# A transformer layer with routed experts on one core: two units share one routed part, norms are split between ACT and POOL, products fill a wait of PE

## The chip, the cores and the metric

The kernel runs on one core of a Trainium2 chip. The metric is the device time of one execution, in microseconds (us); lower is better. Three runs of the kernel before took 269.41, 272.25 and 278.97 us, median 272.25 us. The change is judged against that median.

## The reference, cut to what matters

All arithmetic is float32, on x of 4 batches of 1024 tokens of 64 features.

```
q, k, v = x@Wq+bq, x@Wk+bk, x@Wv+bv
y = ((d_gamma * (q @ k.T)) @ v) @ Wo + bo        # per batch, 1024 x 1024, no softmax
h = where(y >= 0, y, a*y)
n = layernorm(h)                                  # state-space block, 128 states
u = (1-A) * (n@Wb+bb) * (n@Wx+bx),  A = exp(-softplus(n@Wd+bd))
s_t = A_t * s_(t-1) + u_t                         # scan over the 1024 tokens
h = h + ((n@Wc+bc) * s) @ Wy + by
n = layernorm(h)                                  # 16 experts, top 2 by a gate
p = softmax(n@gate_w + gate_b);  top 2, renormalised
h = h + sum over the 2 experts of p_e * (silu(n@w1_e) * (n@w2_e)) @ w3_e
```

## The kernel before, in words

The tokens are cut into four **units** of 1024 rows each (two batches by half of the tokens: `UNITS`, `unit_of`). Every unit goes through attention (8 steps; a step is a product `scores`, L699, a multiplication on DVE, `mix`, L1029, and a product `pv`, L713), then through a chain: `center1`, sums of squares and their root, `turn_norm`, four products of the state-space block (`product`, L739), the scans on DVE, `ssm_out` (L768), and then `center2` (L774, with the raw gate logits, L778), the second norm, the choice of two experts, `count` and `place`.

Each engine runs one instruction queue in program order and waits on semaphores. The order is written out by hand: a loop over **beats** (`for m in range(BEATS)`); two beats are one attention step. `BEAT` gives each operation of a unit its beat after the end of the unit's last step (first number; the second one is for the last unit), and `due(name, m)` says for which units it is due. The chain of unit u thus lies among the attention steps of unit u+1.

The first three units are **routed**: `place` and `give_slots` work out for each token and each of its two experts a slot in a buffer in device memory. A part's buffer has 32 blocks of 128 slots: one block that belongs to each of the 16 experts (own blocks) and 16 that are handed out to whichever expert overflows (shared blocks, `SHARED = 2 * UT`). POOL scatters the normed rows into the slots (`scatter`, L490, 16 indirect transfers a unit), SP loads four blocks at a time (`load_slots`, L379), and this **group** of four blocks goes through PE as `turn_slots` (L822), `hidden` (L858) and, three groups later, `result` (L881). ACT does the silu (L587) and moves results out (L593), DVE multiplies (`gated`, L1158), SP stores results (L400), and POOL gathers them back (`gather`, L499, again 16 transfers a unit). Before, each routed unit is a part of its own: `PARTS = 3`, 8 groups a part, `ROUTED = 24` groups. The owners of the shared blocks are worked out in `spread`, `owner_rows` and `owners`; SP loads the weights of shared blocks by these numbers (`load_weights`, L394).

The last unit is **dense**: all 16 experts on all rows, in 32 groups (`hidden_dense`, L904, and `result_dense`, L916), after the routed groups. Its rows are first multiplied with the share that each expert gets (`weigh`, L1170), which SP spreads over the partitions through device memory (`spread_given`, L414, eight transfers of 512 KB).

A group is cut into four **pieces** (`expert_piece`). From beat `FFN_BEAT` on, `FFN_RATES` says how many pieces are run in each beat among the last unit's chain; what is left runs after the beats. SP stores results 7 groups behind the load (`STORE_LAG`), but only 4 behind at the first group of a part in `LATE_PARTS`. POOL's order is three scatters and then three gathers (`POOL_ORDER`). `COMBINE_AFTER` gives the groups behind which DVE adds gathered results (`combine`, L1193 to L1195).

A second norm before: ACT squares 512 columns into `squares` (L531), DVE sums them (`norm_var`, L1039), ACT takes the root (L535), DVE takes the reciprocal and scales the rows into `n2` (`norm_scale`, L1049).

Of the kernel before, what the change touches and what calls it, by code (L numbers as in the profile page):

```python
# [14 lines left out]
P = 128  # L15
# [15 lines left out]
PARTS = UNITS - 1  # L31
OWN, SHARED = NE, 2 * UT
BLOCKS = OWN + SHARED
GB = 4
PAIRS = GB // 2
GROUPS = BLOCKS // GB
OWN_GROUPS = OWN // GB
SHARED_GROUPS = SHARED // GB
ROUTED = PARTS * GROUPS

# [15 lines left out]
    "relu": (0, 0), "sq1": (2, 2), "std1": (2, 3), "tanh_table": (3, 9), "turned": (9, 6), "tanh": (9, 7),  # L56
    "keep": (13, 8), "half": (26, 21), "sqrt_table": (12, 13), "sq2": (17, 14), "std2": (18, 14), "h": (21, 13),
    "center1": (3, 2), "turn": (6, 6), "d": (7, 7), "x": (9, 8), "b": (10, 9), "c": (12, 11), "out": (15, 13),
    "center2": (17, 14), "turn_h": (22, 11), "count": (25, 18), "owner_row": (32, 24), "prelu": (2, 1),
    "var1": (4, 3), "scale1": (5, 3), "xs": (9, 8), "bx": (11, 9), "scan0": (13, 9), "scan1": (13, 11),  # L60
    "read": (13, 11), "residual": (15, 11), "var2": (18, 13), "scale2": (19, 14), "logits": (20, 14),
    "mark0": (21, 15), "one0": (22, 15), "mark1": (23, 15), "one1": (23, 17), "place": (25, 18), "slots": (27, 18),
    "spread": (31, 19), "owners": (33, 26), "weights": (33, 20), "x_turn": (1, 20), "dispatch": (0, 22),
    "given_turn": (1, 23),
# [3 lines left out]
PV_LAG = 3  # L68
# [23 lines left out]
COMBINE_AFTER = (29, 31, 40, 47, 49, 53)  # L92
# [32 lines left out]

def out_order():
    order = []
    routed = [("routed", r, m) for r in range(PARTS) for m in range(COMBINES)]
# [10 lines left out]
def build_layer(nc, xT, dgT, wqk, vecs, wssm, wgate, rows, wvo, wy, w12, w3, out):  # L139
    with ExitStack() as ctx:  # L140
# [6 lines left out]
        slots_dram = [nc.dram_tensor(f"slots{r}", [BLOCKS * P, D], F32).ap() for r in range(PARTS)]  # L147
        given_dram = nc.dram_tensor("given", [BH, NE, CW], F32).ap()
        results_dram = [nc.dram_tensor(f"results{r}", [BLOCKS * P, D], F32).ap() for r in range(PARTS)]
# [6 lines left out]
        mixed = sb("mixed", [P, 2, BH, CW])  # L156
# [40 lines left out]
        block_at = sb("block_at", [SHARED, NE])  # L197
        iota_i = sb("iota_i", [P, NE], I32)
# [12 lines left out]
        first_slot = sb("first_slot", [P, NE])  # L211
        slot_f = sb("slot_f", [P, 2, UT])
        slot_i = sb("slot_i", [P, PARTS, 2, UT], I32)
        is_past = sb("is_past", [SHARED, NE])
        owner_col = sb("owner_col", [SHARED, 1])
        owner_i = sb("owner_i", [1, PARTS * SHARED], I32)
# [10 lines left out]
        back_v = sb("back_v", [P, PARTS, UT, 2, D])  # L227
# [46 lines left out]
        diff_done, half_done = sem("diff_done"), sem("half_done")  # L274

        scattered = [sem(f"scattered{i}") for i in range(PARTS)]
# [5 lines left out]
        gathered = [sem(f"gathered{i}") for i in range(PARTS * COMBINES)]  # L282
# [53 lines left out]
        def _(sp):  # L336
# [46 lines left out]
            def load_weights(r, i):  # L383

                if i == 0:
                    sp.wait_ge(owner_done, r + 1)
                k = r * SHARED_GROUPS + i
# [3 lines left out]
                if r >= 1:  # L391
                    sp.wait_ge(hid_done, (r - 1) * GROUPS + OWN_GROUPS + i + 1)
# [4 lines left out]
            def store_results(n):  # L397
                r, g = divmod(n, GROUPS)
# [20 lines left out]
            for n in range(ROUTED):  # L419
                r, g = divmod(n, GROUPS)  # L420
# [5 lines left out]
                if 1 <= g <= SHARED_GROUPS:  # L426
                    load_weights(r, g - 1)
# [26 lines left out]
        def _(pool):  # L454
# [22 lines left out]
            link(pool.memset(first_slot[:, 0:1], 0.0))  # L477
            link(pool.memset(chosen[:, UT, :], 0.0))
            link(pool.iota(iota_i[:, 0:NE], [[-1, NE]], NE, 0))
            link(pool.tensor_copy(rank_of[:, :], iota_i[:, 0:NE]))  # L480
            link(pool.iota(iota_i[:, 0:NE], [[P, NE]], 0, P))
            pool.tensor_copy(block_at[:, :], iota_i[0:SHARED, 0:NE]).then_inc(consts, 1)

            def scatter(r):
                pool.wait_ge(zeroed, 16 * PARTS)
                pool.wait_ge(norm_done[1], r + 1)
                pool.wait_ge(slot_done, r + 1)
                for i in range(UT):
                    for k in range(2):
                        pool.indirect_dma_start(  # L490
                            out=slots_dram[r], out_offset=bass.IndirectOffsetOnAxis(ap=slot_i[:, r, k, i:i + 1], axis=0),
                            in_=n2[:, r % 2, i, :], in_offset=None).then_inc(scattered[r], 16)

            def gather(r):
                for i in range(RES_BUFS):
                    pool.wait_ge(stored[i], 16 * ((r + 1) * GROUPS // RES_BUFS))
# [810 lines left out]
```

## Time and profile before

| | |
|---|---|
| median of three runs | 272.25 us (269.41 to 278.97) |
| the profiled execution, its own time | 265.82 us |
| its span, first to last instruction | 264.1 us |
| PE busy | 242.3 us (92%) |
| DVE busy | 164.2 us (62%) |
| ACT busy | 104.4 us (40%) |
| POOL busy | 98.7 us (37%) |
| mean granted clock of PE | 0.947 |

The page shows busy shares over the whole span. PE is busy nearly throughout, but busy is not full speed: the row PEclk, over 40 slices of 6.6 us, shows 5 in four slices from 185 us on in tenths of full speed. The queries by stretch and by time, of which rows stand below, say where that begins and what PE did before it.

### The profile page before, as it was taken

How to read it: one execution, taken by the hardware profiler on the slowest of the kernel's cores; microseconds unless marked ns; L12 is line 12 of the kernel's file. 1: busy time of each engine (PE TensorE's matmuls, PEld its weight loads, DVE VectorE, ACT ScalarE, POOL GpSimd, SP SyncE). 2: the span in 40 equal slices, each digit the busy share in tenths (PEclk: the TensorE clock that was granted, in tenths of full speed). 3: DMA queues.
4: the chain of work that ended last, by engine and by line, in shares of the span. 5: the costliest groups of instructions: out<-in, count | busy, mean ns of one | idle time of the engine just before them, and what ended most of it. 6: DMA issues, size and time to landing. Idle time of an engine off the chain costs nothing.

```text
span 264.1 us, 4634 instructions
## 1 busy us (share of the span) xinstructions
PE 242.3 (92%) x1641; PEld 143.3 (54%) x1641; DVE 164.2 (62%) x289; ACT 104.4 (40%) x186; POOL 98.7 (37%) x119
## 2 busy tenths in 40 slices
PE   8999999999999999966999899599999978999994
PEld 7642224224422442235768688488888644565661
DVE  1354366598999998978695854111214479765773
ACT  2212234603570347037838846323234233334341
POOL 5000000000006774477407777772377517770000
PEclk9999999999999999999999999955559999999999
DMA  5999990000000001434135466554799952112001
GB/s 162 354 381 386 249 206 14 0 0 1 2 0 10 25 27 39 117 100 123 35 84 128 135 158 145 124 135 118 156 242 236 240 125 54 38 25 45 22 21 40
DMA packets 46373, 29.73 MB, mean 113 GB/s; under 512 B 33072, under 2 KB 41456, under 8 KB 45840
## 3 DMA queue, kind: packets, MB, share of 16 engines
q1 hardware_dynamic: 43280, 26.30, 38.5%
q0 software_dynamic: 3072, 3.15, 4.9%
q8 instruction: 13, 0.21, 0.3%
q14 instruction: 8, 0.07, 0.1%
HBM read 20.46 MB, written 8.98 MB: 111 GB/s over the span
## 4 chain that ended last, share of the span: by engine, by line
PE 64%; DVE 16%; issue 8%; DMA 5%; ACT 5%; DVEq 0%; SPq 0%; POOL 0%; ACTq 0%; POOLq 0%
PE ring L858 10%; PE ring L699 9%; PE acc L713 9%; PE turn L881 9%; PE ring L904 7%; DMA results<-res 4%; PE side L739 3%; PE turn L916 3%; DVE state L1070 3%; DVE mixed L1029 2%; DVE dg L1170 2%; PE side L672 2%; PE ring L656 2%; PE acc L822 2%; DVE act L1158 2%
## 5 line engine op out<-in xcount | busy, mean ns | idle before, releaser
L490 POOL DMA_INDIRECT slots<-n,slot_i x48 | 48.1, 1003 | 105.4 <-DVE slot_i L1134 91.7
L1158 DVE TENSOR_TENSOR act<-ring,silu 128x512 f32<-128x512 f32 x56 | 38.5, 688 | 52.0 <-ACT silu L587 51.2
L499 POOL DMA_INDIRECT back_v<-results,slot_i x48 | 46.6, 972 | 31.2 <-DMA results<-res 17.5
L587 ACT ACTIVATE silu<-ring 128x512 f32<-128x512 f32 x56 | 33.3, 597 | 48.9 <-PE ring L904 28.9
L1029 DVE TENSOR_TENSOR mixed<-ring,dg 128x1024 f32<-128x1024 f32 x32 | 39.0, 1218 | 11.8 <-PE ring L699 11.6
L699 PE MATMUL ring<-kq 64*128 64x512 f32 x128 | 35.5, 631 | 0.0
L713 PE MATMUL acc<-mixed,v 128*64 128x512 f32 x128 | 34.5, 617 | 0.6 <-ACT nT L522 0.4
L881 PE MATMUL turn<-w_sb,act 128*128 128x64 f32 (+1 forms) x192 | 31.7, 317 | 1.2 <-ACT res L593 0.9
L881 PEld LDWEIGHTS turn<-w_sb,act 128*128 128x128 f32 x192 | 28.1, 225 | 7.2 <-issue 5.8
L904 PE MATMUL ring<-nT,w_sb 64*128 64x256 f32 x128 | 21.7, 415 | 3.5 <-DVE dg L1170 2.7
L699 PEld LDWEIGHTS ring<-kq 64*128 64x128 f32 x128 | 10.1, 185 | 19.7 <-issue 14.5
L739 PE MATMUL side<-nT,wssm_sb 64*128 64x512 f32 x64 | 17.5, 625 | 3.4 <-ACT nT L543 1.4
L904 PE MATMUL ring<-dg,w_sb 64*128 64x256 f32 x128 | 19.1, 376 | 0.0
L858 PE MATMUL ring<-slots_t,w_sb 64*128 64x128 f32 x192 | 17.5, 334 | 0.8 <-DVE act L1158 0.8
L713 PEld LDWEIGHTS acc<-mixed,v 128*64 128x64 f32 x128 | 6.4, 134 | 21.2 <-issue 15.6
L521 ACT ACTIVATE hT<-acc,vec 128x512 f32<-128x512 f32 x4 | 2.7, 687 | 37.3 <-PE acc L713 37.3
L858 PEld LDWEIGHTS ring<-slots_t,w_sb 64*128 64x128 f32 x192 | 15.0, 233 | 3.9 <-issue 2.8
L904 PEld LDWEIGHTS ring<-nT,w_sb 64*128 64x128 f32 x128 | 10.3, 185 | 12.4 <-DVE dg L1170 8.1
L593 ACT ACTIVATE res<-turn 128x256 f32<-128x256 f32 x24 | 9.2, 383 | 19.7 <-PE turn L881 16.8
L858 PE MATMUL ring<-slots_t,w_shared 64*128 64x128 f32 x192 | 16.3, 317 | 0.1
L858 PEld LDWEIGHTS ring<-slots_t,w_shared 64*128 64x128 f32 x192 | 13.9, 217 | 2.5 <-issue 2.4
L822 PE MATMUL acc<-ident,slots 128*128 128x128 f32 x48 | 11.0, 315 | 2.8 <-DMA slots<-slots 2.8
(144 smaller groups left out, 290.2 us busy)
## 6 DMA issues: line engine op xcount, KB each, us to landing
dg<-dgT SPq DMA_DIRECT2D x8, 512.0 KB, 7.6
dg<-given SPq DMA_DIRECT2D x8, 512.0 KB, 10.2
slots<-zeros SPq DMA_DIRECT2D x3, 1024.0 KB, 13.4
slots<-slots SPq DMA_DIRECT2D x24, 128.0 KB, 2.8
w_shared<-w SPq DMA_DIRECT2D x48, 64.0 KB, 2.1
results<-res SPq DMA_DIRECT2D x24, 128.0 KB, 2.7
w_sb<-w SPq DMA_DIRECT2D x2, 1024.0 KB, 14.5
xs<-xT SPq DMA_DIRECT2D x4, 256.0 KB, 6.4
```

The lines of the kernel that those rows point to most:

```text
L490: pool.indirect_dma_start(out=slots_dram[r], out_offset=bass.IndirectOffsetOnAxis(ap=slot_i[:, r, k, i:i + 1], axis=0), in_=n2[:, r % 2, i ...
L499: pool.indirect_dma_start(out=back_v[:, r, i, k, :], out_offset=None, in_=results_dram[r], in_offset=bass.IndirectOffsetOnAxis(ap=slot_i[: ...
L587: s.activation(silu[:, n % 2], hidden_banks(n)[:, :, 0:PAIRS * P], ACT.Silu).then_inc(silu_done, 1)
L699: mm = pe.matmul(ring[:, 2 * (step % 2) + b, :], kq[rows_b(b), hh, 0, j * P:(j + 1) * P], kq[rows_b(b), hh, 1, th * CW:(th + 1) * CW], sta ...
L713: mm = pe.matmul(acc[rows_b(b), :], v[:, u // 2, j, b, :], mixed[:, step % 2, b, :], start=j == 0, stop=j == JT - 1)
L739: mm = pe.matmul(side[:, b, :], wssm_sb[rows_b(b), col:col + CH], nT[rows_b(b), :], start=True, stop=True)
L822: mm = pe.transpose(slots_bank[:, q * P:(q + 1) * P], slots[:, n % SLOT_BUFS, 2 * q:2 * q + 2, :].rearrange("p n d -> p (n d)"), ident[:, :])
L858: mm = pe.matmul(hidden_banks(n)[:, b, c:c + P], w[:, part * HID:(part + 1) * HID], slots_t[rows_b(b), n % 2, q, :], start=True, stop=True)
L881: mm = pe.matmul(result_bank(n)[:, k * D:(k + 1) * D], act[:, n % ACT_BUFS, k % 2, k // 2 * P:(k // 2 + 1) * P], w, start=True, stop=True)
L904: mm = pe.matmul(hidden_banks(n)[:, b, part * PAIRS * P:(part + 1) * PAIRS * P], w12_sb[rows_b(b), e, part * HID:(part + 1) * HID], x, sta ...
L1029: dve.tensor_tensor(mixed[:, step % 2], ring[:, r:r + 2, :], dg[:, u % 2, j, :].unsqueeze(1).broadcast_to([P, BH, CW]), ALU.mult).then_inc ...
L1158: dve.tensor_tensor(act[:, n % ACT_BUFS], hidden_banks(n)[:, :, PAIRS * P:2 * PAIRS * P], silu[:, n % 2], ALU.mult).then_inc(act_done, 1)
```

## The change

Units 0 and 1 become one routed part. Its buffer keeps 16 own blocks and has 32 shared ones, 12 groups; unit 2 is the second part with 8 groups. `ROUTED` falls from 24 to 20, `ALL_GROUPS` from 56 to 52. Unit 1's tokens go on filling the blocks that unit 0 began (`room`, `past_own`, `moved`, `is_behind`). `load_slots` of the first part waits for the scatters of both units. In detail:

- For units 0 to 2 ACT squares 64 columns at a time with a sum (`accum_out`), eight instructions for one, and DVE's `norm_var` is left out, in both norms.
- In the second norm of units 0 to 2 ACT copies the centred rows to `n2` (`take_raw`), and POOL scales them (`scale_rows`) ahead of the scatter; DVE only takes the reciprocal. `turn_h` waits for `raw_taken`.
- `keep_busy(50)`: ahead of group 12's transposes PE does 50 products of constants, 128x128 in bf16, and only then waits for that group's slots.
- Two `scores` and two `pv` steps are put next to each other, with three buffers for `mixed`.
- `BEAT`, `FFN_BEAT`, `FFN_RATES`, `COMBINE_AFTER` have new values.

```diff
-PARTS = UNITS - 1
+ROUTED_UNITS = UNITS - 1
+PART_UNITS = ((0, 1), (2,))
+PARTS = len(PART_UNITS)
+SHARED = tuple(2 * UT * len(units) for units in PART_UNITS)
+GROUPS = tuple((OWN + n) // GB for n in SHARED)
+ROUTED = sum(GROUPS)
...
+    "relu": (0, 1), "sq1": (2, 2), "std1": (4, 3), "tanh_table": (9, 15), "turned": (6, 6), "tanh": (9, 8),
+    "keep": (12, 10), "half": (27, 22), "sqrt_table": (14, 10), "sq2": (17, 13), "std2": (17, 13), "h": (23, 10),
+    "center1": (3, 3), "turn": (7, 4), "d": (8, 8), "x": (9, 9), "b": (10, 10), "c": (14, 11), "out": (16, 12),
+    "center2": (18, 14), "turn_h": (19, 9), "count": (24, 42), "owner_row": (33, 30), "prelu": (1, 0),
+    "mark0": (21, 13), "one0": (21, 19), "mark1": (22, 22), "one1": (22, 22), "place": (23, 30), "slots": (23, 34),
...
+MIX_BUFS = 3
+PV_LAG = 2
-LATE_PARTS = (2,)
-FFN_BEAT = 66
-FFN_RATES = (2, 2, 0, 1, 2, 2, 5, 4, 3, 4, 1, 4, 3, 2, 4, 4, 2, 4, 3, 4, 4, 4, 5, 2)
+LATE_PARTS = (1,)
+BUSY = 50
+FFN_BEAT = 67
+FFN_RATES = (3, 2, 0, 0, 2, 2, 4, 4, 3, 4, 1, 3, 3, 2, 6, 5, 1, 3, 2, 1, 2, 5, 5, 0)
-COMBINE_AFTER = (29, 31, 40, 47, 49, 53)
+COMBINE_AFTER = (19, 25, 39, 43, 45, 49)
...
+def scores_at(m):
+    step = m // 2 if m % 4 == 2 else (m + 1) // 2
+    return [step] if m % 4 in (2, 3) and 0 < step < ALL_STEPS else []
+def pv_at(m):
+    step = 2 * (m // 4 - 1) + m % 4
+    return [step] if m % 4 < 2 and 0 <= step < ALL_STEPS else []
...
             def load_slots(n):
-                r, g = divmod(n, GROUPS)
+                r, g = part_and_group(n)
                 if g == 0:
-                    sp.wait_ge(scattered[r], 16 * 2 * UT)
+                    for u in PART_UNITS[r]:
+                        sp.wait_ge(scattered[u], 16 * 2 * UT)
...
+            def scale_rows(u):
+                pool.wait_ge(raw_taken, u + 1)
+                pool.wait_ge(scale_done, u + 1)
+                pool.tensor_tensor(n2[:, u % 2], n2[:, u % 2], stats[:, 1, 2, :].unsqueeze(2).broadcast_to([P, UT, D]),
+                                   ALU.mult).then_inc(norm_done[1], 1)
...
+                for i in range(UT):
+                    last = s.activation(squares[:, i, :], bank[:, i * D:(i + 1) * D], ACT.Square, accum_out=stats[:, which, 0, i:i + 1])
+                last.then_inc(var_done[which], 1)
+            def take_raw(u):
+                if u >= 2:
+                    s.wait_ge(scattered[u - 2], 16 * 2 * UT)
+                s.activation(n2[:, u % 2].rearrange("p i d -> p (i d)"), side[:, 1, :], ACT.Copy).then_inc(raw_taken, 1)
...
             def turn_h(u):
-                pe.wait_ge(norm_done[1], u + 1)
+                pe.wait_ge(raw_taken, u + 1)
+                pe.wait_ge(var_done[1], u + 1)
...
             def turn_slots(n):
-                pe.wait_ge(ld_slots[n % SLOT_BUFS], 16 * (n // SLOT_BUFS + 1))
                 if n >= 1:
                     pe.wait_ge(sin_done, n)
+                if n == GROUPS[0]:
+                    keep_busy(BUSY)
+                pe.wait_ge(ld_slots[n % SLOT_BUFS], 16 * (n // SLOT_BUFS + 1))
...
             def place(u):     # second unit of a part
+                dve.tensor_tensor(ranks_sb[:, :, :], turn[:, 0:n + NE].rearrange("p (i e) -> p i e", e=NE),
+                                  row_of(total, UT + 1), ALU.add).then_inc(count_read, 1)
...
+                link(dve.tensor_tensor(added[:, :], n_int[:, :], past_own[:, :], ALU.subtract))
+                link(dve.tensor_tensor(moved[:, :], first_slot[:, 1, :], behind_all[:, :], ALU.subtract))
+                link(dve.tensor_tensor(is_behind[:, :, :], ranks, row_of(room, UT), ALU.is_ge))
+                link(dve.tensor_tensor(is_behind[:, :, :], is_behind[:, :, :], row_of(moved, UT), ALU.mult))
...
+                link(dve.tensor_tensor(slot[:, :, :], slot[:, :, :], is_behind[:, :, :], ALU.add))
```

## Rows read from the trace of the kernel before

**Rows 1.** The page, PE's granted clock in 40 slices, tenths of full speed.
```profile
PEclk9999999999999999999999999955559999999999
```
**Rows 2.** Busy time by stretch: stretch, length, then engines, PEclk, DMA share, GB/s.
```profile
158.00:167.60 9.60, 9.58 (x102) 8.21 (x98) 3.89 (x9) 5.44 (x13) 6.71 (x8) 1.00 0.59 131
167.60:170.40 2.80, 0.00 (x0) 0.00 (x0) 0.00 (x0) 1.01 (x1) 1.89 (x3) 1.00 0.73 163
170.40:198.60 28.20, 28.12 (x174) 24.37 (x174) 4.15 (x6) 8.56 (x19) 15.10 (x16) 0.52 0.70 163
```
**Rows 3.** PE in order of time: the transposes of successive groups, at either clock.
```profile
161.84 0.39 PE L822 MATMUL acc<-ident,slots 128*128 128x128 f32 x2
164.19 0.39 PE L822 MATMUL acc<-ident,slots 128*128 128x128 f32 x2
...
183.03 0.63 PE L822 MATMUL acc<-ident,slots 128*128 128x128 f32 x2
...
187.37 0.63 PE L822 MATMUL acc<-ident,slots 128*128 128x128 f32 x2
```
**Rows 4.** PE in order of time: attention steps and a state-space product.
```profile
45.22 1.13 PE L699 MATMUL ring<-kq 64*128 64x512 f32 x4
46.18 1.02 PE L739 MATMUL side<-nT,wssm_sb 64*128 64x512 f32 x4
47.14 1.08 PE L713 MATMUL acc<-mixed,v 128*64 128x512 f32 x4
...
68.07 1.13 PE L699 MATMUL ring<-kq 64*128 64x512 f32 x4
69.13 1.08 PE L713 MATMUL acc<-mixed,v 128*64 128x512 f32 x4
```
**Rows 5.** PE in order of time: unit 1's second centring, the first group's transposes.
```profile
89.74 1.16 PE L774 MATMUL side<-center_m,hT 128*128 128x128 f32 x8
...
118.11 0.42 PE L822 MATMUL acc<-ident,slots 128*128 128x128 f32 x2
```
**Rows 6.** POOL in order of time: unit 0's last scatter, unit 1's first and last.
```profile
101.80 0.99 POOL L490 DMA_INDIRECT slots<-n,slot_i  x1 [0.30 <-issue]
108.79 0.96 POOL L490 DMA_INDIRECT slots<-n,slot_i  x1 [5.99 <-DVE slot_i L1134]
...
127.81 0.96 POOL L490 DMA_INDIRECT slots<-n,slot_i  x1 [0.31 <-issue]
```
**Rows 7.** DMA issues, 80 to 170 us: KB each, median us to landing.
```profile
slots<-slots SPq DMA_DIRECT2D x18, 128.0 KB, 2.8
...
slots<-n,slot_i POOLq DMA_INDIRECT x48, 2.2
```
**Rows 8.** SP's queue in order of time, around the last part and the spreading.
```profile
159.66 7.86 SPq L400 DMA_DIRECT2D results<-res  x4
167.62 1.03 SPq L379 DMA_DIRECT2D slots<-slots  x2
...
189.21 1.12 SPq L414 DMA_DIRECT2D dg<-given  x2
```
**Rows 9.** Groups by shape: line, shapes, count, busy us, mean ns, idle before.
```profile
L593 ACT ACTIVATE res<-turn 128x256 f32<-128x256 f32 x24 | 9.2, 383 | 19.7 <-PE turn L881 16.8 <-DMA results<-res 3.0
...
L1039 DVE TENSOR_REDUCE stats<-squares 128x8 f32<-128x512 f32 x8 | 5.5, 683 | 2.7 <-ACT squares L531 2.7
...
L531 ACT ACTIVATE squares<-side 128x512 f32<-128x512 f32 x4 | 2.4, 602 | 1.9 <-PE side L774 1.9
...
L472 POOL TENSOR_TENSOR center_m<-center_m,ident 128x128 f32<-128x128 f32 x1 | 0.5, 453 | 0.1
```
**Rows 10.** PE in order of time: the constant products at the start.
```profile
1.22 4.29 PE L656 MATMUL ring<-ones 128*128 128x128 bf16 x50 [1.22 <-POOL ones L463]
...
6.03 1.29 PE L656 MATMUL ring<-ones 128*128 128x128 bf16 x20
```
**Rows 11.** The chain of waits: start, length, what it went through.
```profile
200.16 10.98 DMA results<-res
```

More of the change, by code:

```diff
@@ L55 @@
 BEAT = {
[L56 to L64, printed above, removed]
+    "relu": (0, 1), "sq1": (2, 2), "std1": (4, 3), "tanh_table": (9, 15), "turned": (6, 6), "tanh": (9, 8),
+    "keep": (12, 10), "half": (27, 22), "sqrt_table": (14, 10), "sq2": (17, 13), "std2": (17, 13), "h": (23, 10),
+    "center1": (3, 3), "turn": (7, 4), "d": (8, 8), "x": (9, 9), "b": (10, 10), "c": (14, 11), "out": (16, 12),
+    "center2": (18, 14), "turn_h": (19, 9), "count": (24, 42), "owner_row": (33, 30), "prelu": (1, 0),
+    "var1": (1, 4), "scale1": (5, 6), "xs": (10, 8), "bx": (11, 10), "scan0": (13, 10), "scan1": (13, 10),
+    "read": (14, 10), "residual": (15, 11), "var2": (20, 12), "scale2": (20, 13), "logits": (20, 13),
+    "mark0": (21, 13), "one0": (21, 19), "mark1": (22, 22), "one1": (22, 22), "place": (23, 30), "slots": (23, 34),
+    "spread": (32, 35), "owners": (33, 39), "weights": (39, 31), "x_turn": (1, 21), "dispatch": (1, 37),
+    "given_turn": (5, 35),
 }
@@ L122, with weights_at @@
 EARLY_PIECES = sum(len(expert_pieces_at(m)) for m in range(BEATS))
+def weights_at(n):
+    r, g = part_and_group(n)
+    early = [SHARED_NO[n + OWN_GROUPS - 1]] if 1 <= g <= OWN_GROUPS else []
+    late = [SHARED_NO[n + 1]] if g + 1 >= 2 * OWN_GROUPS and g + 1 < GROUPS[r] else []
+    return early + late
 def out_order():
     order = []
-    routed = [("routed", r, m) for r in range(PARTS) for m in range(COMBINES)]
+    routed = [("routed", r, m) for r in range(ROUTED_UNITS) for m in range(COMBINES)]
     for n in range(ALL_GROUPS + 1):
@@ L145, in sem @@
             return ctx.enter_context(nc.semaphore(name))
-        slots_dram = [nc.dram_tensor(f"slots{r}", [BLOCKS * P, D], F32).ap() for r in range(PARTS)]
+        slots_dram = [nc.dram_tensor(f"slots{r}", [GROUPS[r] * GB * P, D], F32).ap() for r in range(PARTS)]
         given_dram = nc.dram_tensor("given", [BH, NE, CW], F32).ap()
-        results_dram = [nc.dram_tensor(f"results{r}", [BLOCKS * P, D], F32).ap() for r in range(PARTS)]
+        results_dram = [nc.dram_tensor(f"results{r}", [GROUPS[r] * GB * P, D], F32).ap() for r in range(PARTS)]
         xs = sb("xs", [P, HALVES, T])
@@ L656, in warm_up, with keep_busy @@
                     pe.matmul(ring[:, 0, 0:P], ones[:, :], ones[:, :], start=True, stop=True)
+            def keep_busy(n):
+                for i in range(n):
+                    pe.matmul(acc[:, CW - P:CW], ones[:, :], ones[:, :], start=True, stop=True)
             def project_kq(hh, name):
@@ L957, in _ @@
             for m in range(BEATS):
-                if m % 2 == 0 and 2 <= m < 2 * ALL_STEPS:
-                    scores(m // 2)
-                if m >= PV_LAG and (m - PV_LAG) % 2 == 0 and m - PV_LAG < 2 * ALL_STEPS:
-                    pv((m - PV_LAG) // 2)
+                for step in scores_at(m):
+                    scores(step)
+                for step in pv_at(m):
+                    pv(step)
                 if m in PROJ1_BEATS:
@@ L1045, in norm_scale @@
                     dve.wait_ge(turned, u)
-                if which == 1 and u >= 2:
+                if which == 1:
                     dve.wait_ge(scattered[u - 2], 16 * 2 * UT)
```

217 lines of the change are left out of this document (142 added, 75 removed).

## The prediction, made before the change was run

> **What bounds the kernel now.** The page says PE 92% busy, so I read first at what rate it is busy. The row of granted clock [rows 1] is full except for four slices. The stretches [rows 2] show why: PE stands still from 167.60 to 170.40, and then runs 28.2 us at a mean clock of 0.52, that is at 1.2 GHz instead of 2.4 for nearly all of it, although it is busy 28.12 of them. Only then does the clock come back. PE in order of time gives the price: from transposes to transposes a group takes 2.35 us at full clock and 4.34 us at half [rows 3]. The 28.2 us hold 6.5 groups, 15.3 us of work at full clock, so this one spell costs 12.9 us. Ahead of it, 118.1 to 167.6, PE does 16 transposes of groups, 15 hiddens, 13 results and the last unit's chain with few gaps. So PE's work and its clock set the time; DVE shares the bound only while the attention steps of units 1 and 2 run. What has to be read next is where PE will stand still after the change, since one wait of 2.8 us was followed by a spell of ten times its length.
>
> **The change part by part**, against the profiled execution: span 264.1 us, 265.82 with what lies around it. The median of the runs, 272.25, is 6.4 above; I take it that their slow spells were longer, and no trace shows that.
>
> *Four groups less.* 4 x 2.35 = **-9.4 us** at full clock [rows 3]. The loads, silus and stores that go with them are hidden beside PE.
>
> *Pairs of steps.* A lone `scores` takes 68.07 to 69.13 = 1.06 us from start to start; followed by a product of the same shape, 45.22 to 46.18 = 0.96 and then again 0.96 [rows 4]. A pair of `scores` so saves 2.12 - 1.92 = 0.2. For a pair of `pv` no row stands; between 0 and 0.2 by likeness. About 12 of the 16 pairs have nothing else between them: -2.4 to -4.8 us. Against it stands ACT: squares of 512 columns take 602 ns, 256 columns of another function 383 [rows 9], so 0.86 ns a column and 0.16 fixed, 0.22 for 64 columns, eight of them 1.8 us. Bounds: 0.6 (only the columns count) and 3.5 (the sum costs as much again). They replace 0.60 + 0.68, so 0.5 longer in each norm, plus a copy of 0.6 in the second. `turn_h` now waits for them, on PE, once a unit with the next steps queued behind it; its own inputs came earlier before. I put 0.8 us a unit against the pairs. DVE loses six sums (4.1 us) and three row scalings and gains about 3 us of small operations in `place` and `keep_room`. Together **-2 us** up to the last `pv` (-5 to +3).
>
> *Scaling on POOL.* A quarter of that size takes 0.453 there [rows 9], so 1.8 us, between 0.5 (all of it fixed) and 1.8. POOL idles 5.99 us ahead of unit 1's scatter [rows 6]; the scaling fits in there: 0. Without that cover it would delay the scatter by itself.
>
> *The first part has to wait for unit 1.* This is the step I hold to be decisive. Before, group 0 needs only unit 0, whose last scatter is issued at 101.8, and PE comes to it at 118.11 [rows 5, 6]. Now it needs unit 1. From unit 1's `center2` (89.74) to its first scatter go 19.05 us. The new beats pull `place` and `slots` up: out of that chain go the row scaling and a sum (1.4), an operation of the state-space block and one multiplication of a step (2.5, from DVE's operations of 1,024 columns); into it come the copy and longer squares on ACT (1.1) and some seven more small operations (1.7). That leaves 17 to 18; as the choice is also done in denser order I take 16.5, between 14.5 and 19. With 2 us gained in front: 89.74 - 2 + 16.5 = 104.2. The sixteen transfers take 127.81 - 108.79 = 19.0 from first to last issue, the last lands 2.2 later, SP's load 2.8 after that [rows 6, 7]: **128 us** for group 0, 10 later than before. By then PE has done `center1` of the last unit and nothing more, since `turn_slots(0)` stands at beat 67 and the queue behind it (`turn_norm`, the last unit's products, all groups) waits. `center1` will be later than in the trace of before, because relu now follows the squares and the copy in ACT's queue; PE arrives at about 119 to 120. It then stands for some **8 us** (5 to 11). This costs **+10 us** from 118.1 (the 2 us in front are in it), less 1.1 for `center1` that is then done.
>
> *The wait at group 12.* SP stores result 8 before it loads group 12, as it stored result 12 before group 16: four stores at 159.66 to 167.52, the load at 167.62 [rows 8], a wait of 2.8. In that wait PE now does 50 constant products. Twenty took 1.29 us at the start, so 50 take 3.2, or 4.3 as the first fifty did [rows 10]: **+0.4 us** over the wait (0 to 1.5). If PE does not stand still there, the spell behind it goes: **-12.9 us**.
>
> *What is late next.* The last groups then go at full speed into the spreading: eight transfers of 512 KB, first issued at 189.21 [rows 8], and the stores of results queued behind them, of which one landed only after 10.98 us and held ACT and then PE [rows 11]. The transfers need as long as before, PE comes to them sooner. I put **+3 us** (0 to 7). The gathers start later and two of them run back to back, 20 us each (16 x 1.25), but by my dates they end some 5 us before DVE needs them: 0.
>
> Sum without a slow spell: 264.1 + 10 - 1.1 - 9.4 + 0.4 - 12.9 + 3 = 254.1, and with the 1.7 around the span 255.8 us.
>
> *The new slow spell.* PE stands longest at group 0, and a wait of 2.8 us was enough before [rows 2]. So I expect half clock from about 128. How long? The spell of before had only groups in it, with operands of 64 and 128 columns. Here the last unit's products of 512 columns, `center2` and `ssm_out` come among the groups. If that brings the clock back within some 9 us, it costs 9 x (1 - 2.35/4.34) = 4 us; if as late as before, 12.9. I take 4, since the mix resembles the attention steps, at which the clock was never low [rows 1]. Forecast **260 us**, own range 254 to 266.
>
> The Trainium skill, "TensorE: Matmul & The Clock Gate", Part 1, states that a throttled clock is the default and that sustained activity releases it, and the page's closing table warns of idle gaps between bursts. By that rule the change trades one gap for a longer one, and both would be followed by a short ramp only. The trace agrees with the gap and not with the short ramp: 28 us went by at full business.
>
> **The rivals.**
>
> *A, slower: the clock stays low through the whole first part.* Place: from group 0 at 128 until the constant products at group 12. There are 39 us of schedule at full clock (49.5 - 9.4 - 1.1), 36 of them PE's, which become 66: +30, and +2 for the constants at half clock: 255.8 + 32 = **288 us**. It decides the other way from the length of the spell: 2% above 272.25 is 277.7, 21.9 above the sum, which is 48 us of half clock. For it: nothing in the groups raised the clock for 28 us, and the median of the runs hints at more. Against it: the 512-column products.
>
> *B, the spell lasts as long as before.* 255.8 + 12.9 = **269 us**, no change. For it: the only length that is measured.
>
> *C, the gate is not where I see it.* If the route of unit 1 ends 6 to 8 us sooner than I work out, PE hardly stands, no spell follows and the time is 255.8 - 8 = **248 us**. Against it: POOL's sixteen issues alone are 19.0 us.
>
> *D, the constants do not hold the clock at group 12* (the wait is longer than they are, or the rest of the schedule stalls at the spreading): the old spell stays behind a new short one, 260 + 12.9 = **273 us**, no change.
>
> **How the numbers follow.** Chances: forecast 0.40, A 0.20, B 0.17, C 0.13, D 0.10. A run of this kernel tells about 2% from no change: 266.8 and 277.7. Faster: the forecast nearly whole (0.38), C (0.13) and a little of B (0.03): 0.54. Slower: A (0.20) and the upper edges of B and D (0.05): 0.25. The rest, 0.21, is within 2%. The range takes the forecast's own range, most of C, B and D whole and the shorter half of A: 250 to 284, with about 0.1 left out on either side.
>
> **What would show it.** In the trace after: group 0's first L822-like transposes at 125 to 131 us, with PE idle 5 to 11 us before them, released by the slot load. PEclk near 0.5 behind that wait, and the length of it: under 12 us for the forecast, 28 for B, until group 12 for A. At group 12 fifty bf16 products of 3 to 5 us and a full clock behind them. Twenty groups 2.35 us apart at full clock. ACT's eight squares 1.8 us together. PE waiting at `turn_h` about 0.8 us. After the last routed group a wait of ACT for a store. I am wrong if PE does not stand before group 0, or if the clock stays full through that wait.

## The result, and the profile of the changed kernel

The changed kernel takes 276.18 us in the median of 20 runs (273.2 to 293.8), the kernel before 270.43 in 20 runs beside it. The ratio is 1.0365, 95% interval 1.031 to 1.0419: 3.7% slower, where I had forecast 4.5% faster. This and every ratio below compare only the faster executions of both kernels, since some executions of each, the kernel before above all, run a few per cent longer at a lower mean clock. The profiled execution of the changed kernel took 273.29 us, its span is 271.6, 7.5 above the 264.1 of before.

From the page of the changed kernel, busy time and PEclk (40 slices of 6.8 us):

```profile
span 271.6 us, 4573 instructions
...
PE 238.1 (88%) x1585; PEld 143.9 (53%) x1585; DVE 160.5 (59%) x286; ACT 107.7 (40%) x267; POOL 101.6 (37%) x123
...
PEclk9999999999999999996589998589955599999999
```

PE is busy 4.2 us less than before and the span is longer. PEclk has three dips where [rows 1] has one. The stretches of the changed kernel say where (busy of PE, PEld, DVE, ACT, POOL, then the granted clock, DMA share, GB/s):

```profile
126.00:130.60 4.60, 0.02 (x2) 0.04 (x1) 3.61 (x11) 0.90 (x2) 1.95 (x2) 0.50 0.28 70
130.60:137.50 6.90, 5.82 (x35) 4.38 (x37) 2.33 (x10) 3.63 (x6) 0.00 (x0) 0.50 0.38 101
137.50:143.00 5.50, 4.46 (x34) 2.35 (x32) 3.99 (x10) 3.98 (x6) 2.60 (x3) 0.99 0.45 117
...
164.60:167.00 2.40, 0.04 (x1) 0.01 (x1) 0.37 (x1) 0.38 (x1) 0.00 (x0) 1.00 0.52 118
...
169.00:176.30 7.30, 7.07 (x39) 6.29 (x40) 3.21 (x9) 2.30 (x5) 0.00 (x0) 0.50 0.35 80
176.30:180.30 4.00, 4.00 (x53) 4.00 (x51) 0.71 (x4) 0.60 (x1) 0.00 (x0) 0.72 0.56 130
180.30:190.70 10.40, 10.31 (x113) 8.75 (x111) 3.89 (x9) 4.90 (x13) 0.00 (x0) 1.00 0.45 116
...
193.60:196.30 2.70, 0.00 (x0) 0.03 (x1) 0.32 (x1) 0.38 (x1) 0.00 (x0) 0.88 0.85 197
196.30:213.40 17.10, 17.10 (x102) 14.97 (x102) 3.82 (x6) 4.69 (x10) 12.30 (x13) 0.50 0.99 224
```

The second and the third dip come behind a stand of PE, at 164.6 and 193.6. The first is there already at 124, behind stands of 1.51 and 1.86 us, and the longest one, from 126 on, falls into it. PE in order of time shows what it stood for (idle time and releaser in brackets), and the constants:

```profile
123.97 2.04 PE L805 MATMUL turn<-center_m,hT 128*128 128x128 f32 x8 [1.86 <-DVE owner_i L1286]
130.59 0.66 PE L906 MATMUL acc<-ident,slots 128*128 128x128 f32 x2 [4.58 <-DMA slots<-slots]
...
162.12 0.39 PE L906 MATMUL acc<-ident,slots 128*128 128x128 f32 x2
...
167.02 0.41 PE L906 MATMUL acc<-ident,slots 128*128 128x128 f32 x2 [2.38 <-DMA slots<-slots]
...
176.26 4.06 PE L733 MATMUL acc<-ones 128*128 128x128 bf16 x50
180.16 0.39 PE L906 MATMUL acc<-ident,slots 128*128 128x128 f32 x2
```

Group 0 comes at 130.59 (118.11 before [rows 5]), 2.6 after my 128. The clock is at half before the constants and at full behind them; whether they raised it, this trace can't say. Group 10, at 167.02, is the new thing. SP's queue in the changed kernel says why:

```profile
156.24 2.47 SPq L442 DMA_DIRECT2D w_shared<-w  x4
158.76 0.58 SPq L448 DMA_DIRECT2D results<-res  x1
159.39 0.50 SPq L427 DMA_DIRECT2D slots<-slots  x1
160.65 2.47 SPq L442 DMA_DIRECT2D w_shared<-w  x4
163.16 0.58 SPq L448 DMA_DIRECT2D results<-res  x1
163.79 0.50 SPq L427 DMA_DIRECT2D slots<-slots  x1
164.97 2.49 SPq L442 DMA_DIRECT2D w_shared<-w  x4
...
168.68 7.74 SPq L448 DMA_DIRECT2D results<-res  x4
176.52 1.02 SPq L427 DMA_DIRECT2D slots<-slots  x2
...
197.56 1.13 SPq L462 DMA_DIRECT2D dg<-given  x2
```

From one load of slots to the next go 163.79 - 159.39 = 4.4 us, where PE takes 2.35 a group. SP issues the four weight transfers, each with its owner's address, in 2.47, a store in 0.58, slots in 0.50, and 0.7 to 0.8 go before the weights. So the slots of group 10 are issued at 163.79, and PE gets them at 167.02. It could have been read beforehand; the same queue in the kernel before:

```profile
142.83 0.50 SPq L379 DMA_DIRECT2D slots<-slots  x1
144.17 2.47 SPq L394 DMA_DIRECT2D w_shared<-w  x4
146.70 0.58 SPq L400 DMA_DIRECT2D results<-res  x1
147.33 0.50 SPq L379 DMA_DIRECT2D slots<-slots  x1
```

It is 4.5 us a group there too, but only four groups of eight brought weights, and while SP was at it PE had the last unit's products among its groups and took 3.2 to 4.1 us for each. With units 0 and 1 as one part, eight groups of twelve bring weights, and PE is down to 2.35 us before SP is through the second four of them.

**One sum closes.** Group 0 is 12.5 us later. From it to the first group of the last part go 49.6 us (52.3 before), from there to the first transfer of the spreading 17.4 (18.8). So the spreading starts at 197.56 instead of 189.21 [rows 8], 8.35 later, and from it to the end go 74.0 us, before 74.9. 8.35 - 0.9 = 7.5. The changed kernel ran those 74 us at clock 0.50 until 216, and yet they are no longer than before.

### The profile page after: what moved, and what is told of

The parts are those of the page before. It is cut to its first block, busy times and chain, and to the rows that moved or that the text cites. A ratio compares the mean times of both kernels' runs of the same rounds, so it can differ in the third digit from the quotient of the medians.

```text
span 271.6 us, 4573 instructions
## 1 busy us (share of the span) xinstructions
PE 238.1 (88%) x1585; PEld 143.9 (53%) x1585; DVE 160.5 (59%) x286; ACT 107.7 (40%) x267; POOL 101.6 (37%) x123
## 4 chain that ended last, share of the span: by engine, by line
PE 57%; DVE 17%; SPq 9%; issue 7%; ACT 6%; DMA 2%; DVEq 0%; POOL 0%; ACTq 0%; POOLq 0%
PE ring L988 10%; PE acc L790 8%; PE ring L776 7%; SPq L442 6%; PE ring L942 5%; PE turn L965 4%; PE side L818 4%; PE turn L1000 3%; DVE mixed L1114 2%; PE ring L728 2%; DMA slots<-slots 2%; PE side L749 2%; ACT squares L595 2%; DVE drive L1148 2%; DVE dg L1309 2%
## 5 line engine op out<-in xcount | busy, mean ns | idle before, releaser
L1297 DVE TENSOR_TENSOR act<-ring,silu 128x512 f32<-128x512 f32 x52 | 35.7, 688 | 52.1 <-ACT silu L657 51.6
L657 ACT ACTIVATE silu<-ring 128x512 f32<-128x512 f32 x52 | 31.1, 597 | 45.0 <-PE ring L988 28.9
L776 PE MATMUL ring<-kq 64*128 64x512 f32 x128 | 33.4, 617 | 0.0
L965 PE MATMUL turn<-w_sb,act 128*128 (+1 forms) x160 | 27.3, 325 | 1.0 <-ACT res L663 1.0
L965 PEld LDWEIGHTS turn<-w_sb,act 128*128 128x128 f32 x160 | 24.2, 232 | 4.4 <-issue 3.0
L536 POOL TENSOR_TENSOR n<-n,stats 128x512 f32<-128x512 f32 x3 | 3.2, 1051 | 58.3 <-DVE stats L1132 58.2
L942 PE MATMUL ring<-slots_t,w_shared 64*128 64x128 f32 x192 | 18.8, 350 | 0.5 <-ACT slots_t L651 0.3
L906 PE MATMUL acc<-ident,slots 128*128 128x128 f32 x40 | 9.5, 326 | 10.3 <-DMA slots<-slots 10.3
L651 ACT ACTIVATE slots_t<-acc 128x256 f32<-128x256 f32 x20 | 7.6, 379 | 16.5 <-PE acc L906 16.4
L988 PEld LDWEIGHTS ring<-dg,w_sb 64*128 64x128 f32 x128 | 12.8, 194 | 1.7
L818 PEld LDWEIGHTS side<-nT,wssm_sb 64*128 64x128 f32 x64 | 5.3, 193 | 15.6 <-DVE drive L1148 8.8
```

The lines of the kernel that those rows point to most:

```text
L657: s.activation(silu[:, n % 2], hidden_banks(n)[:, :, 0:PAIRS * P], ACT.Silu).then_inc(silu_done, 1)
L776: mm = pe.matmul(ring[:, 2 * (step % 2) + b, :], kq[rows_b(b), hh, 0, j * P:(j + 1) * P], kq[rows_b(b), hh, 1, th * CW:(th + 1) * CW], sta ...
L818: mm = pe.matmul(side[:, b, :], wssm_sb[rows_b(b), col:col + CH], nT[rows_b(b), :], start=True, stop=True)
L942: mm = pe.matmul(hidden_banks(n)[:, b, c:c + P], w[:, part * HID:(part + 1) * HID], slots_t[rows_b(b), n % 2, q, :], start=True, stop=True)
L965: mm = pe.matmul(result_bank(n)[:, k * D:(k + 1) * D], act[:, n % ACT_BUFS, k % 2, k // 2 * P:(k // 2 + 1) * P], w, start=True, stop=True)
L988: mm = pe.matmul(hidden_banks(n)[:, b, part * PAIRS * P:(part + 1) * PAIRS * P], w12_sb[rows_b(b), e, part * HID:(part + 1) * HID], x, sta ...
```

## The experiments

Two theories at first. **Theory 1:** SP's order of issue makes PE wait for slots, and the clock falls behind each wait; without it the forecast holds. **Theory 2:** the loss is the later group 0 and the work, and the waits only show it. Four of the six chips were disturbed: the kernel before takes 360 us there instead of 267 to 270, and PE and ACT stall for 14 us and more where the profile names no wait of either program. The changed kernel never ran there unedited, so the ratios from these chips are compared only with each other. In the lines shown, L906, L907 and L899 are the transposes of a group and L965, L957 and L958 its results; the numbers shift with the edits.

**The changed kernel, unedited**, twice where the kernel before takes 267 and 269 us.

> The changed kernel itself, unedited, on the chips on which the other experiments run. In the seven experiments so far the kernel before took 360 us instead of 270, with waits of up to 13 us on ACT, DVE and PE that no semaphore of the program explains. If the cause of the loss (three waits of PE for slots, each followed by half clock) is the same here, the ratio is near 1.04. If those foreign waits cover it, the ratio is near that of the experiments that leave the slot loads alone (0.975 to 0.98), and only differences between kernels of one call can be read.

> The changed kernel, unedited, so that the next kernels can be set against it on the same chip. On a chip where the kernel before takes about 267 us: 274 to 278. Where the kernel before takes 360 us, as in three of the calls: theory 1 (SP's queue carries the loss) says ratio 0.975 to 0.985, beside 0.95 for the two kernels with a relieved queue; theory 2 says 0.95, as theirs.

277.73 us (ratio 1.0399, 1.0318 to 1.0481) and 276.26 (1.0343, 1.0273 to 1.0414). The result repeats. In the first, the clock fell already at 109, in the wait of 3.28 us for `drive`, and the spreading came at 202.34. PE had no wait for slots at group 10 there, its longest gap in the 6 us before was 0.7 us, and still the clock was at half from about 163 to 183. So the second spell doesn't need the wait at group 10.

**Front: pairs alone, in the kernel before.**

```diff
-                mm = pe.matmul(acc[rows_b(b), :], v[...], mixed[:, step % 2, b, :],
+                mm = pe.matmul(acc[rows_b(b), :], v[...], mixed[:, step % MIX_BUFS, b, :],
...
+ scores_at(m), pv_at(m) as in the change, three buffers
```

> The kernel before with scores and pv in pairs and three buffers for mixed, nothing else of the change. Theory (a pair of equal products saves 0.2 us, two pairs a four-beat, and only place and slots ahead of the state-space operations ate that in the changed kernel): the last pv of unit 3 ends 3 to 5 us sooner than 116.2 us, the time falls by 2 to 5 us. Rival (DVE sets the pace of the steps, pairs or not): no change, last pv within 1 us.

270.01 us beside 267.02, ratio 0.9985 (0.9931 to 1.0039): no difference. The last `pv` ended about 1 us sooner (the row behind it starts at 115.09, before 116.18), and the spreading started at 190.54, not sooner: three waits for slots (0.26, 2.70, 2.14) took it back. So pairs save about 1 us up to the last `pv`, not the 2.4 to 4.8 of my sum, and none of it reaches the end.

**No constants; light weights; no late part.** The first two edit the changed kernel, the third the kernel before. Light weights leave out that a shared block gets the weights of its owner, so the result is not the layer's.

```diff
-BUSY = 50
+BUSY = 0
...
-                for j in range(GB):
-                    sp.dma_start(w12_shared[rows_b(j % 2), k % WEIGHT_BUFS, j // 2, :],
-                                 w12[bass.ds(owner[j] * D, D), :])...
+                for j in range(PAIRS):
+                    sp.dma_start(w12_shared[:, k % WEIGHT_BUFS, j, :], w12[2 * j * D:(2 * j + 2) * D, :])...
...
-LATE_PARTS = (2,)
+LATE_PARTS = ()
```

> The changed kernel without the 50 constant products ahead of group 12 (BUSY = 0); in the changed kernel they took 4.06 us and stood at 176.3 us, in the middle of a stretch at half clock that ended with them. Theory 1 (they bring the clock back): the stretch at half clock that began at about 168 goes on through the 8 groups behind it, some 20 us more at half clock less the 4 us they took: +5 us or more against the changed kernel, 277 us in its profile. Rival (the wait for group 12's slots was there anyway and the clock would come back by itself): within 2 us of the changed kernel.

> The changed kernel, but the weights of a shared group come in two transfers of 128 rows from fixed rows instead of four of 64 rows by owner, and SP reads no owners: the same bytes, half the issues. It leaves out that the shared blocks get their owner's first weights. Theory 1 (SP's issue time, 4.4 us a shared group against 2.35 on PE, makes the waits of 2.38 us at group 10 and 2.72 us at group 17): both waits shrink below 1 us, the slow stretches behind them (168 to 178 and 196 to 216) go, and the time falls by 10 to 16 us, to some 257 us in the profile. Rival (the bytes on the DMA engines make the slots late): no change, within 2 us.

> The kernel before with LATE_PARTS = (): SP stores 7 groups behind the load at the first group of the last part too, so the load of group 16 no longer stands behind the stores of results 10 to 12. Theory (the wait of 2.84 us came from SP's order, and the 28.2 us at half clock from the wait): the wait goes, PEclk stays full, and the time falls by 2.8 + 12.9 less 3 to 7 lost to the spreading's transfers: 9 to 13 us. Rival A (the slots of unit 2 are late for another reason): the wait stays, no change. Rival B (the clock falls for another reason than the wait): the wait goes and the slow stretch stays, -3 us.

All on disturbed chips. No constants: 0.9782 (0.9631 to 0.9934). Light weights: 0.9454 (0.9332 to 0.9575), on two other chips 0.9481 and 0.9458. No late part: 0.9812 (0.9726 to 0.9899), on another chip 0.9827. The wait of 2.84 us ahead of group 16 is gone in its traces, though PE is slower there anyway, and the gain is about half of what I expected. Set against each other, light weights are worth 3% more than the changed kernel without constants; that pointed to SP, but light weights lower both issue and reads of owners.

**Groups later; `place` later.** Both edit the changed kernel.

```diff
-FFN_RATES = (3, 2, 0, 0, 2, 2, 4, 4, 3, 4, 1, 3, 3, 2, 6, 5, 1, 3, 2, 1, 2, 5, 5, 0)
+FFN_RATES = (0, 0, 0, 0, 0, 3, 2, 4, 4, 4, 1, 3, 3, 2, 6, 5, 1, 3, 2, 1, 2, 5, 5, 0)
...
+    late = 4 if name in ("place", "slots") else 0      # units 0 and 1 only
```

> The changed kernel with the first pieces of groups at beat 72 instead of 67, so that turn_norm, count and the last unit's first product stand ahead of the wait for group 0 in PE's queue, and 7 pieces fewer before the end of the beats. Theory (what costs most at the gate is what is queued behind it): PE does some 2 to 4 us of work inside the wait, the pure wait before group 0 shrinks from 4.58 to under 2, the last unit's chain runs ahead, and the time falls by 2 to 6 us; the clock may stay up. Rival (the last unit's chain is hidden beside the groups anyway, only total work counts): within 1 us, since the same work is merely done earlier and the chain's own waits take its place.

> The changed kernel with place and slots of units 0 and 1 four beats later, behind the next unit's first two state-space operations on DVE. Theory (PE waits 2.08 and 3.26 us for drive L1148 because DVE runs place and slots first): both waits go, the last pv of unit 3 ends 4 to 5 us sooner than 117.8; the scatter of unit 1 starts 0 to 4 us later than 106.3, so group 0 comes at 130 to 135 and the end moves by -1 to +4 us. Rival (the front is what sets the time): the end moves by -4 us. Rival 2 (DVE's load as a whole makes those waits): the last pv does not move.

0.9754 (0.9683 to 0.9825) and 0.9788 (0.971 to 0.9865), disturbed chip. With the later `place` no wait for `drive` is over 1.5 us, but PE waits for slots in six places, 13.0 us in all, 5.9 of them ahead of group 0: what it gains in front it gives back there. Neither ratio differs from that without constants, and neither shows what its edit is worth. With `place` later for unit 2 as well, the queues wait for each other for ever, so that kernel has no time.

**SP's queue relieved, bytes unchanged**: stores issued by ACT, or weight loads at other groups.

```diff
+ACT, take_result(n), behind the copy:
+                s.wait_ge(res_read, n + 1)
+                s.dma_start(results_dram[r][...], res[:, n % RES_BUFS]).then_inc(stored[n % RES_BUFS], 16)
...
-WEIGHT_BUFS = 4
+WEIGHT_BUFS = 6
+LOAD_AT = (1, 2, 3, 4, 5, 6, 9, 10, 11, 12, 14, 15)   # load k behind the slots of this group
```

> The changed kernel; the only difference is that the stores of results are issued by ACT right behind the copy that fills them, no more by SP, so that SP no longer holds slots and weights back for them. Theory 1 (the order of SP's queue: 4.4 us of issue per shared group of the first part, 0.58 of it the store, and at group 12 four stores that wait for result 8): a shared group then takes 3.8 us on SP, so PE still waits for slots in the first part, but by about 1 us instead of 2.4; at group 12 the wait is under 3 us and lies wholly under the fifty constants; at group 17 it is under 1 us and the last half-clock spell is missing or shorter. Time 8 to 12 us below the 276 of the changed kernel, 264 to 268. Theory 2 (bytes, or the work of the chain, set the waits; the queue only shows them): waits as before and 274 to 278.

> The changed kernel with six weight buffers instead of four, which lets SP load the weights of shared blocks at other groups: behind the slots of groups 1 to 6, 9 to 12, 14 and 15 instead of 1 to 4, 7 to 10 and 13 to 16. Same transfers, same bytes. Theory 1 (SP's queue): the run of four groups at 4.4 us on SP is broken up while PE is still slowed by the last unit's chain, so the wait of 2.4 us ahead of group 10 goes, the spell of 9 us with it, and the waits at groups 16 and 17 fall below 1 us: 266 to 271. Theory 2: 274 to 278.

> The kernel before, with the stores of results issued by ACT right behind the copy that fills them. SP then loads the slots of group 16 as soon as their buffer is free instead of behind the store of result 12 (167.52 us). Theory 1: the wait of 2.8 us ahead of group 16 and the 28 us at half clock behind it go: 12 to 15 us less than the kernel before, 252 to 256, unless the waits behind it (group 17 on, now 0) take its place; then 262 to 270. Theory 2 (the wait is that for the scatters of unit 2 or for the buffer, which the store only hides): no change, 266 to 272.

Disturbed chip, in this order: 0.9505 (0.9462 to 0.9548) and 0.9532 (0.9468 to 0.9596); the kernel before with stores by ACT 0.9865 (0.9792 to 0.9938), less than I expected of it. Then beside the unedited changed kernel (276.26), where the kernel before takes 268.73:

> The changed kernel with the stores of results issued by ACT behind the copy that fills them. Theory 1: 2 to 4% below the unedited changed kernel beside it, the fifty constants are behind a wait of under 3 us at group 12. Theory 2: within 1% of it.

> The changed kernel with six weight buffers instead of four and the loads of shared weights behind the slots of groups 1 to 6, 9 to 12, 14 and 15. Theory 1 (order of SP's queue): 2 to 4% below the unedited changed kernel beside it. Theory 2 (bytes or the chain's work): within 1% of it.

Stores by ACT: 273.61, ratio to before 1.0257 (1.0164 to 1.035); this interval and that of the unedited kernel (1.0273 to 1.0414) overlap. Weights spread: 271.37, 1.0064 (0.9935 to 1.0193). The intervals of weights spread and of the unedited kernel do not meet: by the ratios it is 2.7% faster, by the medians 1.8%, and it can't be told apart from the kernel before. Only two of its four executions are in the ratio. Waits of PE on that chip, in us, times and longest, unedited kernel:

```profile
PE acc L906 <- DMA slots<-slots: 8.5, 4, 2.6
```

and with the weights spread:

```profile
PE acc L907 <- DMA slots<-slots: 2.8, 2, 1.9
```

The wait at group 10 is gone and so is that at group 17. Same bytes, other order: SP issues the slots of group 10 at 160.51 instead of 165.52, and Theory 1 is right on the waits. It is wrong on the clock:

```profile
161.97 2.02 PE L943 MATMUL ring<-slots_t,w_shared 64*128 64x128 f32 x16 [0.44 <-ACT slots_t L652]
...
183.77 0.39 PE L907 MATMUL acc<-ident,slots 128*128 128x128 f32 x2
```

The clock is at half from 162 until the constants, behind gaps of 0.58, 0.34 and 0.44 us, and group 12 comes at 183.77, later than in the unedited kernel beside it (182.41). What is won is won behind group 12: group 17 at 197.57 instead of 198.98, the first transfer of the spreading at 197.88 instead of 200.59. This profile is of the longest of the four executions (274.3 us; the unedited kernel's took 276.27). So 5 us (medians) to 7 us (ratios) came back, not the 16 by which I was wrong.

**Both, without constants.** With no wait at group 12 there is nothing for them to fill.

> The changed kernel with both edits to SP's work (stores issued by ACT; six weight buffers and the loads spread) and without the fifty constants, which then would have no wait to fill. Theory 1: PE waits for slots nowhere behind group 0, so the only spell at half clock is the one behind group 0 (about 13 us) and the time is my forecast's, 258 to 264 on a chip where the kernel before takes 267, 4 to 6% below the unedited changed kernel anywhere. Theory 2: within 1% of it.

269.75 us, 1.0076 (0.999 to 1.0163), 2.4% under the unedited kernel by the medians and no better than the kernel before. Theory 1 fell here: it wanted 258 to 264. The profile is of the longest execution, 276.49 us, and the other three took 268.2 to 270.34. For that reason the same wait with stores by ACT alone comes first; its profiled execution took 273.76 us, beside a median of 273.61:

```profile
PE turn L957 <- ACT res L651: 12.3, 2, 11.7
```

Both edits: PE's waits, then its last transposes of a group:

```profile
PE turn L958 <- ACT res L652: 14.3, 2, 13.7
...
PE acc L899 <- DMA slots<-slots: 1.9, 1, 1.9
```

```profile
194.80 0.39 PE L899 MATMUL acc<-ident,slots 128*128 128x128 f32 x2
```

The last group comes 10.7 us sooner (205.47 in the unedited kernel beside it), as it should, and then PE stands 13.7 us. With stores by ACT alone it comes at 194.42 and PE stands 11.7. The clock rose at 173 here without any constants. SP's queue and the chain of waits of the same kernel:

```profile
191.02 5.03 SPq L457 DMA_DIRECT2D dg<-given  x8
```

```profile
193.06 23.10 DMA results<-res
```

And its stretches:

```profile
187.00:204.00 17.00, 15.35 (x156) 12.78 (x153) 4.66 (x7) 7.50 (x16) 12.67 (x14) 1.00 0.87 187
204.00:217.00 13.00, 0.00 (x0) 0.00 (x0) 2.83 (x5) 0.98 (x2) 9.96 (x11) 0.63 1.01 224
```

All DMA engines are busy at 224 GB/s. The eight transfers of 4 MB went out in one row, and a store of 128 KB behind them took 23.1 us, while PE waited for its buffer. With stores by ACT alone the store issued at 192.68 took 23.2. With the weights spread the stores stand between the transfers. The last group comes about as soon behind the first transfer there (4.4 us, with stores by ACT 3.5), and PE stands 3.12 us for the result. What the three shorter executions with both edits did at this place, no trace shows.

**The last four stores back on SP, between the transfers.** From both edits above, one thing undone.

```diff
             for i in range(GIVEN_LOADS):
                 spread_given(i)
+                store_results(ROUTED - GIVEN_LOADS + i)
```

> e11 (stores by ACT, weight loads spread, no constants) with one thing undone: the stores of the last four routed results are issued by SP again, one behind each pair of transfers of the spreading, as in the kernel before. In e11 SP issued all eight transfers of 512 KB from 191.02 on in 5 us; the store of a result issued at 193.06 landed after 23.1 us and PE stood still for 13.7 us. Theory 3 (the spreading became the bound once the routed groups came 10 us sooner, because eight transfers in a row stand ahead of the small stores): with the stores between them PE waits 2 to 5 us at that place, no spell at half clock follows, and the time is 9 to 12 us under e11's 269.75: 257 to 261 where the kernel before takes 267 to 269, ratio 0.96 to 0.975. Rival (4 MB at the 207 to 236 GB/s seen there take 18 to 20 us whoever issues what, so PE has to wait for the spreading itself or for the gathers beside it): the wait moves to the multiplication with the shares or to the last stores, 266 to 270, ratio 0.99 to 1.01.

It ran on a disturbed chip only: 339.92 us, ratio 0.9279 (0.9187 to 0.937), the lowest of all kernels run on such chips (0.9454 to 0.9865) and the only one whose interval ends under 0.94. The kernel that it undoes one thing of never ran on such a chip. In its trace no wait for a result is over 0.6 us, but a stall of 19.8 us stood between the first and the second pair of transfers, so the trace can't confirm the mechanism. Whether it beats the kernel before on an undisturbed chip is open; the disturbed chips don't tell, as stores by ACT and weights spread had the same ratio there (0.9505 and 0.9532) and 1.0257 and 1.0064 on the other.

## Why the prediction was wrong

The spans and SP's queue give a number that I had not looked for. From the first transfer of the spreading to the end:

| kernel | spreading starts | span | from it to the end |
|---|---|---|---|
| before | 189.21 | 264.1 | 74.9 |
| before, with pairs | 190.54 | 266.2 | 75.7 |
| changed | 197.56 | 271.6 | 74.0 |
| changed, again | 202.34 | 276.3 | 74.0 |
| changed, third time | 200.59 | 274.5 | 73.9 |
| weights spread | 197.88 | 272.6 | 74.7 |
| stores by ACT | 190.94 | 272.0 | 81.1 |
| both, no constants | 191.02 | 273.6 | 82.6 |

As long as the stores stood between the transfers, the end was 74 to 76 us behind the start of the spreading. The clock made no difference that shows: in the changed kernel it was at half until 216; in its third execution it was at full from 205 to 215, and PE then stood 3.4 us for a result and 2.4 for the shares. In these traces, what comes ahead of the spreading counts by that one date; no experiment shows why it is so constant. My 255.8 would have needed it at 254.1 - 74.5 = 180, ten us before the date of before.

The same can be read from my sum. It has group 0 at 128.1, group 12 46.2 us behind it (52.3 - 9.4 - 1.1 + 0.4 + 4) and the end 83.8 behind that (93.7 - 12.9 + 3). Measured are 130.6, 49.6 and 91.4: of the 13.5 us 2.5 were lost up to group 0, 3.4 up to group 12 and 7.6 behind it.

- **The first part has to wait for unit 1** (forecast 128, +10): right in kind, 130.59, +12.5. The three stands ahead of group 0 make 7.95 us, as forecast, but at other places. Unit 1's first scatter came at 106.31 instead of 104.2, and PE stood 4.58 us behind a `center1` that itself came 4 us late (123.97).
- **The new slow spell** (+4): right. Half clock from 124 to 137.5, 13 us and not 28; PE is busy 7.8 us of them, so it costs about 4. The clock came back among the last unit's products, where I had expected it; that it was for them, nothing shows.
- **Constants at group 12**: 4.06 us as forecast, clock full behind them. They came into a spell that was already there. In the four traces where that was so the clock rose while they ran, which points to them but doesn't show it: with both edits to SP and no constants the clock rose by itself at 173.
- **Pairs, -2 up to the last `pv`**: wrong, +1.6 (117.8 against 116.25). Pairs do run 1.94 to 1.99 instead of 2.1. I costed `place` by its own length and not by who queues behind it: DVE runs it from 101.36 to 105.5, ahead of the state-space operation, and PE stood for that (with `place` later, no such wait was over 1.5 us). In the changed kernel:

```profile
78.04 1.13 PE L818 MATMUL side<-nT,wssm_sb 64*128 64x512 f32 x4 [2.08 <-DVE drive L1148]
...
108.32 1.13 PE L818 MATMUL side<-nT,wssm_sb 64*128 64x512 f32 x4 [3.26 <-DVE drive L1148]
```

- **Scaling on POOL, 0**: right; it took 1.05 us, not 1.8. Squares on ACT: 1.55 us for the eight, 1.8 forecast.
- **Four groups less, -9.4, with "The loads, silus and stores that go with them are hidden beside PE"**: this is the step that failed, and it took the -12.9 with it. What PE saves counts only if SP issues the transfers as fast, and it doesn't. Up to group 12 this shows as the wait for slots of 2.38 us at group 10, behind which PE works 7.07 us at half clock, about 3.5 us lost; the spell may come without the wait, as the executions above show. Behind group 12, SP takes 21.0 us from the load of group 12 to the first transfer of the spreading (176.52 to 197.56), with PE at full clock for most of it. In the kernel before it took 21.6 (167.62 to 189.21 [rows 8]), with PE at half clock. Its issues leave no gap over 0.9 us in either. So a faster PE could not bring the spreading forward; it stood 2.72 us at group 17 instead. With the weight loads spread it took 18.1 (179.79 to 197.88), and that edit alone gave back 2.7% of the time.
- **-12.9 for the old spell**: wrong. The spell was not removed, it moved (196 to 216 instead of 170 to 198.6). In the kernel before, 9.4 of its 28.2 us lay behind the start of the spreading, where the clock made no difference. The rest, 8.6 us at most, could not be won while SP's issues set the date of the spreading.
- **Late next: the spreading, +3 (0 to 7)**: right as far as it was put to the test. PE stood 3.6 us in all for results and shares in the kernel before, 7.1 in the third execution of the changed kernel and 6.9 with the weights spread. Only with the stores behind all eight transfers did one wait reach 11.7 to 13.7 us; 4 MB at the 220 GB/s of those stretches are 19 us.

Rivals A to D: none as written. There were three short spells, not one long one (A had PE slow until group 12: it was slow in 17 of those 50 us). D comes nearest, a new short spell and a later one behind it, but the later one came at group 17 and not at group 12. The Trainium skill, "TensorE: Matmul & The Clock Gate", Part 1, has idle gaps followed by a ramp. The three dips behind stands of PE in this trace agree in kind; the spell that began behind gaps of at most 0.6 us with the weights spread does not. The lengths of 13, 10 and 20 us are of this trace alone.

## What to carry to other kernels

Before taking groups out of PE's work, work out the time that the engine that issues the transfers needs for a group: here 4.4 us on SP against 2.35 on PE. Where that engine has no gaps, a faster PE only waits. Look for a date from which the end is a constant (here the first transfer of a 4 MB spread, 74 us from the end), and cost every edit by what it does to that date; here a slow clock behind it cost nothing. A stall removed ahead of a bulk transfer meets the transfer: with the small stores between its parts PE stood 3.4 us at most for a result, with all of them behind it 11.7 to 13.7.

## What the runs showed of the hardware

- The clock behind a wait is not settled by the wait. The changed kernel waited 3.26 us for `drive` at 105 and kept the full clock (1.00 in 110 to 118); in a later execution it waited 3.28 us at the same place and had 0.50 from 109 to 115. With stores by ACT and with both edits PE had the same wait of 0.32 us at 162, and before it much the same 7 us (busy 5.87 of 7.10 and 6.42 of 7.60). In the first the clock stayed full, 1.00 in 162.1 to 173; in the second it was 0.54 in 162.6 to 173.8, at a higher busy share (11.11 of 11.20 against 8.93 of 10.90). Why, no run here tells.
- Issuing a transfer whose address comes from a register took SP 0.62 us (2.47 for four), that of slots or a store at a fixed place 0.50 to 0.58.
- Eight 64-column squares with their sums, each with a read of the accumulator behind it, took ACT 1.55 us, against 0.60 for the one of 512 columns without sums [rows 9].
- A store of 128 KB issued by ACT 1.7 us behind the first of SP's eight transfers of 512 KB took 23.2 us, and in another kernel, 2.0 us behind, 23.1.
